# Eight network stages in one kernel: the attention weights of stages 4 and 6 are turned by VectorE and by transfers inside SBUF

## The reference, cut to what matters

```python
# stage 4: 16 heads, each with a query and key of 128 and a value of 8, on (8, 256, 128)
A = jnp.einsum('bhnd,bhmd->bhnm', q, k) / jnp.sqrt(jnp.float32(Dm))
A = jnp.where(mask[None, None], A, -jnp.inf)
A = jax.nn.softmax(A, axis=-1)
sa = jnp.einsum('bhnm,bhmd->bnhd', A, v).reshape(Bm, Nm, Dm)
...
# stage 6: 16 heads of 64; keep is the selection of keys, FF the running penalty
att = att - FF[:, None]
att = jnp.where(keep[:, None], att, neg_inf)
y = jax.nn.softmax(att, axis=-1) @ v
y = y.transpose(0, 2, 1, 3).reshape(B, T, H * hd)
y = y @ W_proj.T + b_proj
```

## Time and profile before

| | us |
|---|---|
| median of 3 runs | 1315.55 (1311.95 to 1318.73) |
| span of the profiled execution, first to last instruction | 1314.2 |
| TensorE busy | 1262.0 (96%) |
| DVE busy | 927.8 (71%) |
| ACT busy | 901.5 (69%) |
| POOL busy | 777.6 (59%) |

### The profile page before, as it was taken

The page is one execution under the profiler, slowest core; times in us unless marked ns, Lnnn a source line. Parts: engine busy times, 40 slices in busy tenths (PEclk is TensorE's granted clock), DMA queues, the critical chain, the costliest instruction groups (busy, mean ns, idle before and its releaser), DMA issues.

```text
span 1314.2 us, 25939 instructions
## 1 busy us (share of the span) xinstructions
PE 1262.0 (96%) x8634; PEld 888.8 (68%) x8634; DVE 927.8 (71%) x3613; ACT 901.5 (69%) x2507; POOL 777.6 (59%) x853
## 2 busy tenths in 40 slices
PE   8799689999998999999999999999999999999997
PEld 4355356668744777777776777777788877776665
DVE  5979988867768788767656454787597678655254
ACT  6848899968574898766867666376778758765231
POOL 2989987668457867575655855356524524433434
PEclk9769989999998999999999999999999999999999
DMA  8753000110061000111000101101200011002430
GB/s 284 203 131 95 9 1 2 58 58 2 1 197 34 1 2 2 58 73 30 37 2 2 65 1 68 65 2 66 84 3 2 1 62 29 1 1 66 112 98 24
DMA packets 26373, 66.74 MB, mean 51 GB/s; under 512 B 2945, under 2 KB 7809, under 8 KB 25473
## 3 DMA queue, kind: packets, MB, share of 16 engines
q1 hardware_dynamic: 26240, 65.10, 16.4%
HBM read 61.74 MB, written 3.34 MB: 50 GB/s over the span
## 4 chain that ended last, share of the span: by engine, by line
PE 82%; DVE 9%; ACT 4%; POOL 2%; issue 2%; POOLq 0%; DVEq 0%; ACTq 0%
PE bank L1216 71%; PE bank L1220 11%; DVE arena L2126 2%; ACT arena L1668 2%; DVE arena L1935 2%; ACT L1668 1%; DVE stats L1949 1%; DVE arena L2192 1%; DVE stats L1938 1%; POOL arena L2566 1%; ACT bank L1668 1%; DVE arena L2190 1%; ACT X L1668 0%; POOL stats L2489 0%; DVE arena L2204 0%
## 5 line engine op out<-in xcount | busy, mean ns | idle before, releaser
L1668 ACT ACTIVATE arena<-arena 128x256 f32<-128x256 f32 (+4 forms) x804 | 355.6, 447 | 31.8 <-DVE arena L2192 15.0
L1668 ACT ACTIVATE arena<-bank 128x512 f32<-128x512 f32 (+3 forms) x354 | 190.9, 570 | 199.4 <-PE bank L1216 125.0
L1216 PE MATMUL bank<-XT,W 128*128 128x512 f32 (+1 forms) x720 | 287.5, 534 | 0.4 <-DVE arena L2204 0.3
L1216 PEld LDWEIGHTS bank<-W,arena 128*128 128x128 f32 x1888 | 230.2, 193 | 41.1 <-issue 35.7
L2513 POOL TENSOR_TENSOR arena<-arena 128x512 f32<-128x512 f32 (+2 forms) x108 | 171.3, 1600 | 137.5 <-DVE arena L1935 55.1
L1216 PE MATMUL bank<-W,arena 128*128 128x128 f32 (+1 forms) x1888 | 239.1, 277 | 1.1 <-POOL arena L2513 0.7
L1216 PE MATMUL bank<-arena 128*32 128x128 f32 (+8 forms) x2864 | 222.2, 335 | 6.9 <-DVE arena L2192 4.1
L2565 POOL TENSOR_TENSOR arena<-arena 128x256 f32<-128x256 f32 x192 | 118.6, 618 | 169.6 <-DVE arena L2198 169.1
L2566 POOL TENSOR_TENSOR arena<-arena 128x512 f32<-128x512 f32 x192 | 201.0, 1047 | 0.0
L1216 PEld LDWEIGHTS bank<-arena 128*32 128x32 f32 (+4 forms) x2864 | 147.0, 151 | 79.6 <-issue 52.8
L1220 PE MATMUL bank<-CF,arena 128*128 128x128 f32 x1312 | 181.7, 277 | 8.7 <-POOL arena L2566 5.3
(11 more groups left out here) (153 smaller groups left out, 1693.6 us busy)
## 6 DMA issues: line engine op xcount, KB each, us to landing
arena<-rws SPq DMA_DIRECT2D x44, 512.0 KB, 5.7
arena<-rep SPq DMA_DIRECT2D x62, 256.0 KB, 5.4
arena<-rws SPq DMA_DIRECT2D x8, 384.0 KB, 10.9
W<-w SPq DMA_DIRECT2D x1, 2692.0 KB, 9.1
W<-w SPq DMA_DIRECT2D x1, 2316.0 KB, 8.3
W<-w SPq DMA_DIRECT2D x1, 2124.0 KB, 8.8
XT<-wkq SPq DMA_DIRECT2D x4, 512.0 KB, 5.1
W<-w SPq DMA_DIRECT2D x1, 2005.0 KB, 15.0
```

The costliest lines, as they stand in the source:

```text
L1216: return e.matmul(o, lhsT, rhs, start=start, stop=stop, skip_group_check=True)
L1668: return e.activation(o, a, func, **kw)
```

## The change

- Stages 4 and 6 (`SWAPPED`) lose x.tr: 192 steps with 768 TensorE transposes and 192 copies out of PSUM.
- x.ex now leaves the masked scores in PSUM. A new ACT step x.xp reads them there and writes the exponentials to `pexp` with the columns regrouped by 32 (`exps`, `keys_of`).
- x.nm multiplies the same numbers of elements, through access patterns with runs of 32 in place of 128 and 256.
- New DVE step x.tv, two for each unit: transposes 128 partitions x 768 columns in place, in squares of 32x32.
- New SP step x.tx, one for each unit: 16 DMAs from SBUF to SBUF, each 32 partitions x 384 floats (1536 bytes a row, 48 KB in all), from row group i, column group k of `pexp` to row group k of a buffer of 1536 columns (`keyed`): two buffers for a lane in stage 4, one in stage 6 (`K_AT`, `TURNED`). SP waits for both x.tv, and for the x.pv that last read the buffer. x.pv waits for the unit's DMA semaphore (`moved`), x.xp of unit u for the one of unit u-2.
- Stage 6's weights come in three pieces: two (query, key; value) over stages 0, 2 and 3, and the output projection ("late") over stage 4's.
- 6.qk may put its first eviction on ACT too. A new `TURNS` in full: 4.qk on DVE falls from 36 to 24, 6.qk from 32 to 10, 6.v from 14 to 8, 6.pv from 13 to 4, 1.tr from 54 to 48, 1.y from 3 to 0, each of them then on ACT; 4.y on DVE rises from 1 to 2 and f from 35 to 39. The planner's list for TensorE goes from 1273 parts to 1081, for DVE from 1146 to 1131, for ACT from 827 to 780, for SP from 142 to 207.

The diff, without `TURNS` and without changes of addresses:

```diff
+    "1.tv": "V.90", "4.tv": "V.90", "6.tv": "V.90", "1.tx": "D5.4", "4.tx": "D5.4", "6.tx": "D5.4",
...
+SWAPPED = (4, 6)
+TURNED = {1: 2, 4: 2, 6: 1}
...
-OVER = {4: (0,), 5: (1,), 6: (4,), 7: (3, 5)}
+OVER = {4: (0,), 5: (1,), 6: (0, 2, 3), 7: (3, 5)}
...
+        K_AT = {1: (8736, 3072), 4: (7840, 9376), 6: (8800, 8800)}
...
+            if s in SWAPPED:
+                y = keyed(s, c, u).rearrange("p (i w b) -> p w i b", i=4, b=32)
+                return y[:, 3 * j + 2] if kt else y[:, 3 * j:3 * j + 2]
...
+                elif name in ("1.tx", "4.tx", "6.tx"):
+                    on.wait_ge(*after("tv", f"{s}.tv", c, 2 * n))
+                    on.wait_ge(*after("tv", f"{s}.tv", c, 2 * n + 1))
+                    if n >= TURNED[s]:
+                        on.wait_ge(*summed(s, c, n - TURNED[s]))
+                    px, to = pexp(s, c, n), keyed(s, c, n)
+                    for k in range(4):
+                        for i in range(4):
+                            e.dma_start(to[32 * k:32 * k + 32, i * 384:(i + 1) * 384], px[32 * i:32 * i + 32, k * 384:(k + 1) * 384]
+                                        ).then_inc(moved(s, c, n)[0], 16)
+                elif name == "late":
+                    stage_over(4)
+                    e.dma_start(W[0][:, 2071:3223], ws[6][:, 3096:4248]).then_inc(d_w6, 16)
...
+                    if s in SWAPPED:
+                        on.wait_ge(*moved(s, c, n))
+                    else:
+                        for k in range(3):
+                            on.wait_ge(*emptied(u("T", f"{s}.tr", c, n * 3 + k)))
...
+                elif name in ("1.xp", "4.xp", "6.xp"):
+                    unit, h = n // 2, n % 2
+                    nm = small(s, c, unit)
+                    if s == 4:
+                        on.wait_ge(*after("nm", "4.ex", c, n))
+                    if unit >= 2:
+                        on.wait_ge(*after("rec", f"{s}.nm", c, n - 4))
+                        on.wait_ge(*moved(s, c, unit - 2))
+                    for j in (2 * h, 2 * h + 1):
+                        b = u(f"S{j}", "1.sc", c, unit) if s == 1 else u(f"S{j % 2}", f"{s}.ex", c, n)
+                        on.wait_ge(*after("mx", f"{s}.ex", c, n, 2 - 2 * (j % 2)))
+                        act(exps(s, c, unit, j, 0), keys_of(s, bank[b.i][:, 0:128]), ACT.Exp, bias=nm[:, 2 * j:2 * j + 1],
+                            scale=-1.0, accum_out=nm[:, 16 + 2 * j:17 + 2 * j])
+                        act(exps(s, c, unit, j, 1, True), keys_of(s, bank[b.i][:, 128:384]), ACT.Exp, bias=nm[:, 2 * j + 1:2 * j + 2],
+                            scale=-1.0, accum_out=nm[:, 17 + 2 * j:18 + 2 * j]).then_inc(done[b.i], 1)
...
+                elif name in ("1.tv", "4.tv", "6.tv"):
+                    unit, h = n // 2, n % 2
+                    on.wait_ge(*after("pn", f"{s}.nm", c, n))
+                    x = pexp(s, c, unit).rearrange("p (k x) -> p k x", k=4)[:, :, 192 * h:192 * h + 192]
+                    e.transpose(x, x).then_inc(has["tv"], 1)
...
+                    if s in SWAPPED:
+                        px = pexp(s, c, unit)[:, :].rearrange("p (k j x) -> p j k x", k=4, x=96)[:, 2 * h:2 * h + 2]
+                        e.tensor_tensor(px[:, :, :, 0:32], px[:, :, :, 0:32], rec[:, :, 0:1].unsqueeze(3).to_broadcast([128, 2, 4, 32]), ALU.mult)
+                        e.tensor_tensor(px[:, :, :, 32:96], px[:, :, :, 32:96], rec[:, :, 1:2].unsqueeze(3).to_broadcast([128, 2, 4, 64]),
+                                        ALU.mult).then_inc(has["pn"], 1)
+                        continue
```

More of the change, by code:

```diff
@@ L227, in attention @@
             if u >= 2:
-                add(f"{s}.pv", u - 2, *[(f"{s}.tr", (u - 2) * 3 + k) for k in range(3)], *vals(u - 2),
+                moved = [(f"{s}.tx", u - 2)] if s in SWAPPED else [(f"{s}.tr", (u - 2) * 3 + k) for k in range(3)]
+                add(f"{s}.pv", u - 2, *moved, *vals(u - 2),
                     *([(f"{s}.pv", u - 3)] if u >= 3 else []))
@@ L360, in weight_steps @@
 def weight_steps():
-    loads = [("load", s, 0, [need for q in OVER[s] for c in range(NC) for need in ([("f", 0, c, q)] if q else [("0.in", 1, c, 0), ("0.dt", 0, c, 0)])]
+    loads = [("load", s, 0, [need for q in OVER[s] for c in range(NC) for need in ([("f", 0, c, q)] if q else [("0.e", 0, c, 0)] if s == 6 else [("0.in", 1, c, 0), ("0.dt", 0, c, 0)])]
               + [("4.st", n, PREP, 0) for n in range(4) if s == 4]) for s in OVER]
+    loads += [("late", 6, 0, [("f", 0, c, 4) for c in range(NC)])]
     loads += [("4.l", 0, n, [("4.st", n - 2)] if n >= 2 else []) for n in range(4)] + [("4.k", 0, 0, [("4.l", 0)])]
@@ new lines @@
+    3742, 3748), ("7.e", 7, 3): (3754,), ("g", 7, 3): (3756, 3758, 3759), ("load", 4, PREP): (1216,), ("load", 5, PREP): (1893,),
+    ("load", 6, PREP): (1974,), ("load", 7, PREP): (2880,), ("late", 6, PREP): (2596,), ("4.l", 0, PREP): (41, 92, 191, 180),
+    ("4.k", 0, PREP): (72,), ("4.a", 0, PREP): (91, 119, 110, 120, 210, 234, 198, 233), ("4.g", 0, PREP): (143, 148, 127, 131,
+    267, 303, 271, 275), ("4.st", 0, PREP): (170, 149, 306, 312), ("0.a", 0, PREP): (18, 20, 43), ("0.f", 0, PREP): (8, 10),
@@ L808, in network @@
         counts = count_results(order)
+        queries_v = {(name, c, n) for name, _, c, n, _ in order["V"] if name == "6.qk"}
         bank = [ctx.enter_context(nc.psum_tensor(f"bank{i}", [128, 512], F32)) for i in range(8)]
@@ L819, in network @@
         d_l, d_g = [sem(f"d_l{n}") for n in range(4)], [sem(f"d_g{n}") for n in range(4)]
+        d_tx = [[sem(f"d_tx{lane}_{i}") for i in range(2)] for lane in range(LANES)]
+        d_w6 = sem("d_wp6")
         d_wr = [sem(f"d_wr{c}") for c in range(NC)]
@@ L924, in km1, with exps, keys_of, keyed @@
             return ar(c, 6688, 2048)
-        P_AT = {1: (0, 2560), 4: (5280, 6816), 6: (5728, 7264)}
+        P_AT = {1: (0, 1536) if 1 in SWAPPED else (0, 2560), 4: (4768, 6304) if 4 in SWAPPED else (5280, 6816), 6: (5728, 7264)}
+        K_AT = {1: (8736, 3072), 4: (7840, 9376), 6: (8800, 8800)}
         T_AT = {1: (8736, 9248, 9760, 10272, 1536), 4: range(8352, 10912, 512), 6: range(8800, 10848, 512)}
-        M_AT = {1: 10784, 4: 2592, 6: 2592}
+        M_AT = {1: 10784, 4: 2080 if 4 in SWAPPED else 2592, 6: 2592}
         def pexp(s, c, u):
             return ar(c, P_AT[s][u % 2], 1536)
+        def exps(s, c, u, j, t, split=False):
+            px = pexp(s, c, u)
+            if s not in SWAPPED:
+                return px[:, j * 384 + 128 * t:j * 384 + 128 + 256 * t]
+            w = px.rearrange("p (k x) -> p k x", k=4)
+            w = w[:, :, 96 * j + 32 * t:96 * j + 32 + 64 * t]
+            return w.rearrange("p k (w a) -> p k w a", a=32) if t and split else w
+        def keys_of(s, a):
+            if s not in SWAPPED:
+                return a
+            n = a.shape[1] // 128
+            return a.rearrange("p (w k a) -> p k w a", w=n, k=4, a=32) if n > 1 else a.rearrange("p (k a) -> p k a", k=4)
+        def keyed(s, c, u):
+            return ar(c, K_AT[s][u % 2], 1536)
+        def moved(s, c, u):
+            lane = LANE[c]
+            before = TASKS[lane][:TASKS[lane].index((s, c))]
+            units = 4 * sum(k in SWAPPED for k, _ in before) + u // 2 + 1
+            return d_tx[lane][u % 2], 256 * units
         def third(s, c, g):
@@ L1434, in _ @@
                     on.wait_ge(*emptied(u("b", "6.v", c, n)))
-                    for k in range(3):
-                        on.wait_ge(*emptied(u("T", "6.tr", c, n * 3 + k)))
+                    if s in SWAPPED:
+                        on.wait_ge(*moved(s, c, n))
+                    else:
+                        for k in range(3):
+                            on.wait_ge(*emptied(u("T", "6.tr", c, n * 3 + k)))
                     for i in range(2):
@@ L1913, in _ @@
                     act(head0(c, 1, 1), bank[b.i][:, 256:512], ACT.Identity, bias=wt(6, "bk")[:, 0:1]).then_inc(done[b.i], 1)
+                elif name == "6.qk" and p == 0 and (name, c, n) not in queries_v:
+                    b, m = u("b", name, c, n), unit_of(6, n)[1]
+                    on.wait_ge(*after("bq8", "6.a", PREP))
+                    if n >= 2:
+                        on.wait_ge(*filled(u("S1", "6.ex", c, 2 * n - 3)))
+                    on.wait_ge(*filled(b))
+                    for i in fresh6(n):
+                        x = 2 * m + i
+                        ins = act(q6(c, n)[:, i * 256:(i + 1) * 256], bank[b.i][:, i * 256:(i + 1) * 256], ACT.Identity,
+                                  bias=pre[:, 80 + x:81 + x], scale=0.125)
+                    ins.then_inc(done[b.i], 1)
                 elif name == "6.qk":
@@ L2196, in _ @@
                     nm = small(s, c, unit)
-                    on.wait_ge(*after("ex", f"{s}.ex", c, n))
+                    if s in SWAPPED:
+                        for j in range(2):
```

(10 more changed lines are left out.)

112 lines of the change are left out of this document (78 added, 34 removed), and 478 rows, old and new, of tables (EMITS, PARTS, TURNS).

## The result

The changed kernel takes 1560.99 us (median; 1557.86 to 1563.13), the kernel before 1317.14 beside it: a ratio of 1.1861, 95% interval 1.1824 to 1.1898. Forecast were 1251 us and a range up to 1322.

The account below looks back on a forecast made before the run. The prediction took TensorE as the bound, full from 500 to 1200 us: 1314.2 - 90 for removed transposes + 26 for holes = 1250.2 us of span, median 1251; own range 1228 to 1277, overall 1226 to 1322.

Parts of the forecast that it names:

- the price of an issue on SP: SP's new transfers in stages 4 and 6: 0.33 us each, 5.3 us for a unit; other end 0.64 each.
- A unit's weights are there some 7.4 us after SP starts: Stages 4 and 6: 5.3 us of issues plus 2.1 of landing, hidden while other lanes keep TensorE full.
- SP's 339 us: SP's issuing of all units' transfers in stages 4 and 6: 339 us in all; other end 655.
- the holes: TensorE's idle time in the stretch after the change: 13 to 39 us, taken as 26, including longer latency and SP's queue.
- The rival of SP's queue: At the x.tx steps, SP's ordered issues become the bound and the kernel is slower, about 1388 at 0.70 us; chance 0.15.
- the point itself: SP's price for one transfer, 0.63 us, at which 64 units fill the old 740 us stretch; chance 0.04 of landing there.
- the even case: Whole kernel: a time within 0.5% of 1315.5 us, no change that a measurement can tell; chance 0.04.
- The waiting term: SP's waiting at the head of its queue for x.tv: 1.5 us for each unit, in the formula for SP's queue.
- the least period of a lane: Buffers set a minimum of 7 us a unit in stage 4 and nearly 9 in stage 6; neither binds by itself.
- The first 450 us: The start of the kernel, before the full TensorE stretch: claimed to lose and gain nothing that a row shows.
- -90: TensorE, stages 4 and 6: 768 transposes removed at 0.1175 us each save 90 us, with ends 83 and 106.
- DVE's transpose: New DVE step in stages 4 and 6: 128 transposes at 0.90 us, 115 us in all; bad end 2.1 us each.

Follow-up runs that it names:

- the version through DRAM: Changed kernel with a unit's sixteen transfers replaced by four writes to DRAM and one read back: 1389.63 us; with the read as a later task, 1387.52 us.
- fifteen issues behind the one: Changed kernel with one transfer of 128 rows for a unit, exchange left out, then fifteen 256 B transfers into a spare tile nothing reads: 1517.84 us.

## Why the prediction was wrong, point by point

**The step that failed: the price of an issue on SP.** The prediction put it at 0.33 us, since "a transfer of 32 whole rows is nearest to the plain ones", and named the other end, 0.64. It is 0.59. The 0.33 was that of four writes to DRAM and of single loads, the 0.64 that of eight issues back to back. The same rows have a third value that the prediction left out: 2.04 us for four reads back to back into SBUF, 0.51 each. Which likeness sets the price is not shown. It is not the destination alone: the one read of 128 rows in the version through DRAM has SBUF as destination too and took 0.34 us, and the copy of as many bytes from SBUF to SBUF took 0.46. Nor is it the bytes or the rows, by the runs above. In the changed kernel the writes of the expert shares still take 0.30 us each and their reads 0.43, beside the 0.59 of the new kind; only a run of its own gave that price.

**Both of its uses failed with it.** "A unit's weights are there some 7.4 us after SP starts", hidden by other lanes: the way was 11.5. The runs come close to bearing the judgement on 7.4 out (eight transfers at 6.7 us and the 192 B pieces at 6.6 cost nothing; 7.4 itself was not run) and show that 11.5 us is not hidden. And SP's 339 us became 620. In the sum, latency and queue stood together with the holes in 26 us. By the estimate explained below (work is busy time by mean clock), TensorE's idle time rose from 52 to 272 us, by 219, and the time lost to its clock from 32 to 139, by 107, while the work fell by 80: 219 + 107 - 80 = 246, but for rounding the rise of the span from 1314 to 1561.

**The rival of SP's queue had the right kind, place and sign, and the wrong point.** It had a chance of 0.15, and its signs came as listed: issues of 0.59 us back to back, and TensorE idle with a DMA as releaser. It said that from 0.63 us on the kernel loses, with 1.5 us of waiting for a unit; at 0.59 that formula gives 64 x (9.5 + 1.5) = 704 us, still inside the old 740. Counted as the prediction counts, the length of a run of issues by their number, the price is 10.10 / 16 = 0.63 us, the point itself, and the formula gives the time of the kernel before and not 1561. So the right price alone would have brought the forecast to the even case at most. Measured per unit are 10.8 us of issuing (the longer issues, the gaps and the other tasks included) and 3.2 us of waiting, 895 us in all. The waiting term, for which the prediction had no row, was half of what it is: waits at the head of a list kept in strict order were up to 25 us long. Also, time was lost already with twelve transfers, 7.1 us of issues for a unit, where the run with one transfer gives each unit (1166.6 - 539.2) / 64 = 9.8 us: this queue, served in order, holds others up before its issues alone fill it. Of the way as a second cost, the prediction had only the least period of a lane, 7 and 9 us a unit, "so neither period binds by itself".

**How the loss divides.** Load alone costs 222 us (fifteen issues behind the one), a way of 11.5 us alone 186; the two together, as changed, 265. So they cover each other for the greater part, and no sum of separate shares can be given.

**What was left without that loss: 1296 and not 1251.** The run with one transfer has the whole rest of the change. The windows of its trace:

```profile
0.00:500.00 500.00, 440.00 (x2962) 273.69 (x2963) 382.36 (x1258) 369.80 (x933) 339.21 (x307) 0.89 0.24 71
500.00:1180.00 680.00, 661.80 (x4377) 468.47 (x4377) 531.44 (x2192) 474.22 (x1500) 385.90 (x502) 1.00 0.30 110
```

Each row has the length, the busy time of PE, PEld, DVE, ACT and POOL, the clock and the DMAs. From 500 us on the forecast of the holes holds: 18 us of 680, inside the 13 to 39. "The first 450 us lose and gain nothing that a row shows" does not: TensorE is busy 440 us in place of 457 and at a mean granted clock of 0.89 in place of 0.94. As an estimate, busy time by mean clock is the work in full-speed us: 1262.0 x 0.975 = 1230 before and 1208.3 x 0.957 = 1156 here, so the change took 74 us of work off TensorE, 0.097 for each transpose. Idle time rose from 52 to 86 us, by 34, half of it before 500 us, and the time lost to the clock from 1262.0 x 0.025 = 32 to 1208.3 x 0.043 = 52, by 20. -74 + 34 + 20 = -20, from 1314 to 1294. In the forecast stood -90 and +26: the transposes were priced 16 us too high by this, the idle time 8 too low, and the lower clock was not in it. That the new order of the early tasks brings the idle time there is argued only: no run kept the old order beside the new tasks.

**The clock in the changed kernel.** Its mean fell from 0.975 to 0.892, that is, between the levels 2.4 and 1.2 GHz the lower one was granted more often. Two windows of its trace, in the form of the rows above:

```profile
200.00:300.00 100.00, 92.95 (x825) 65.12 (x825) 81.66 (x347) 84.23 (x273) 72.82 (x80) 0.99 0.05 20
700.00:800.00 100.00, 65.72 (x370) 40.44 (x369) 51.25 (x216) 48.43 (x171) 44.62 (x82) 0.81 0.32 79
```

Where TensorE was busy 93 of 100 us the granted clock was 0.99, where it was busy 66 it was 0.81. So the idle time comes with a lower clock, and the loss is larger than the waits: TensorE is busy 1289 us with 768 instructions less than in its 1262 before. By the same estimate as above, 1289.1 x 0.108 = 139 us are lost to the clock, 87 more than with one transfer, and idle time is 272 us, 186 more; with 6 us less of work these are about the 265 us that the transfers cost.

**Right, by its own steps:** 768 transposes gone from the group, 1312 to 544; DVE's transpose 0.964 us for 0.90; POOL's shorter runs no dearer, 1041 ns beside 1047 and 776 us in all as before; ACT -27 us for -25. DVE's busy time rose by 33 us for 15. The masked sum that now goes to PSUM was taken at nothing, and its instructions last 46 us longer; durations overlap in the busy time, so they don't add up to the 33:

```profile
L2314 DVE CUSTOM_DVE_ANT_0 bank<-bank,CB 128x256 f32<-128x256 f32 x128 | 59.4, 464 | 0.0
L2319 DVE CUSTOM_DVE_ANT_0 arena<-bank,CB 128x256 f32<-128x256 f32 x128 | 53.7, 420 | 0.0
L2312 DVE DVE_READ_ACCUMULATOR2_ANT arena<- 128x1 f32 x256 | 35.9, 140 | 0.0
L2319 DVE DVE_READ_ACCUMULATOR2_ANT arena<- 128x1 f32 x128 | 10.6, 83 | 0.0
```

That is 256 x 44 ns for the long form, 256 x 22 for the short (307 ns in the mean for 285) and 512 x 57 for the read of the accumulator behind it. DVE is not the bound, so it cost nothing here. The transfers of a unit overlap, as said: sixteen land in the time of their issues and 1.9 us.

The rule of the Trainium skill's page DMA: Bandwidth & Descriptors (Rules for kernel authors), that transfers under 64 KB pay mostly overhead, came out true in its advice to join them: four transfers of 192 KB took 1294 us, sixteen of 48 KB 1561. The 2 us for each transfer that the prediction takes from the same page stand there for transfers issued from GpSimd; on SP the landing was 1.9 us here, and it overlapped, so it was not what was paid. What was paid was the issuing, 0.59 us each, one behind the other in SP's queue, alike from 256 B to 96 KB.

## What to carry to other kernels

Before a transpose or a copy is traded for small transfers, multiply their count by the price of an issue on the queue that issues them, and measure that price on one unit of the very transfers, since the rows of one kernel hold prices from 0.30 to 0.60 us; add that product to the unit's way as well as to the queue's load. A queue that serves several lanes in a fixed order can cost before its issues fill it (here 5 us of issues for a unit every 10 were free and 7 were not), since in its waits at the head nothing behind is issued. And a latency is free only up to the slack of the order of tasks, here 6.7 us at least and less than 11.5: test it with one slow transfer before building the change.

## What the runs showed of the hardware

- An issue on SP from SBUF to SBUF: 0.59 us back to back, for 256 B, 48, 64 and 96 KB alike, 0.60 for 192 KB, 0.62 for 8 whole rows of 6144 B; 0.46 for a single one of 768 KB. From SBUF to DRAM 0.30 for the writes of the expert shares and 0.44 in the median of the four writes of a unit. From DRAM to SBUF 0.34 for one of 768 KB, 0.43 for the reads of the expert shares and 0.60 for the broadcasts of stage 0. On POOL's queue, SBUF to SBUF, 0.50.
- Landing of one 768 KB transfer inside SBUF, by the size of its pieces: 3.6 us (6144 B), and with one short piece read again and again 5.3 (384 B), 6.6 (192 B), 11.5 (96 B), 14.9 (48 B, with the DMA engines at 98%). With pieces of 96 B, 24 of the 64 issues held SP for over 1 us, up to 9.6.
- A DVE transpose of 128 x 768 float32 in squares of 32: 964 ns, 1.26 ns a column.
- DVE's masked sum with PSUM in place of SBUF as destination: 464 for 420 ns on 256 columns, and 140 for 83 ns for the accumulator's read behind it.
